# Decoder layer on one core: one PSUM bank for the turned probabilities of both heads, two banks for the query and key projections, and a new order of steps

## The chip, the cores and the metric

The kernel runs on one core of one Trainium2 chip. The metric is the device time in microseconds; before the change it is 413.04, the median of three runs (412.48 to 413.12). The core has a matrix engine (TensorE, PE in the profile, its weight loads as PEld), a vector engine (VectorE, DVE), an activation engine (ScalarE, ACT), GpSimd (POOL) and SyncE (SP), which issues most DMAs. Each works through its own instructions in the order written, and they wait for each other through semaphores. Matmul results go to PSUM, which has eight banks; this kernel uses all of them, and a bank must have been copied out before it is written again.

## The reference

```
x = x + attention(layernorm(x))        # 16 heads of 64, rmsnorm inside, softmax over 256 keys, w_out, b_out
x = x + cross(layernorm(x), ctx)       # one head of 128, 512 context rows
x = x + ffn(layernorm(x))              # 128 -> 512 -> 128 with fake quantisation:
                                       #   activations uint8, one scale for the whole tensor (max / 255)
                                       #   weights int8 per output channel (max |w| / 127)
```

x is 8 x 256 x 128, the context 8 x 512 x 128, all float32. The scale of the quantisation is taken over the whole tensor, so the feed-forward part can begin only when all eight batches have left the cross attention.

## The kernel before

The order of all work is written out by hand. A batch has eight **steps** (j = 0 to 7), one for each pair of heads; batch 0 is "first", batches 1 to 6 are "mid" and run in a loop of two batches a turn, batch 7 is "last". In a step TensorE does work for pairs at different stages: it projects queries and keys for the pair three ahead (`project_qk`, six matmuls, L435), makes the scores two ahead (`scores`, twelve, L442), turns the probabilities of this pair (`turn_probs`, four transposes a head, L454), adds the output projection of two pairs back (`project_out`, L471) and multiplies probabilities and values of the pair before (`values`, L462). Projection and scores keep float32 accuracy in three passes with a rounded part (hi) and a rest (lo): ACT copies the rounded part out of the bank (`split_hi`), VectorE subtracts for the rest (`split_lo`), and only then is the bank free.

Around it, for each head: VectorE takes the row maxima (`maxima`), ACT the exponentials with their sums (`exps`), VectorE inverts the sums (`invert_sums`), POOL scales the probabilities (`scale_probs`), TensorE turns them, and VectorE copies the turned ones out of PSUM (`keep_turned`). ACT copies the values' result out as oT (L771) before the output projection can read it.

Each step has two places for a **side task** on one bank, `side_bank`: place 0 after the projection, place 1 after the transposes. PLACE (L52) says which task stands where: W1, W3 (value projections of this batch), V0, V2 and TH (value projections and the transposed input of the next batch), and the cross attention of the batch before: TC (its context transposed), TX (xn2 transposed), QX, SX0, SX1 (scores), PX0, PX1 (transposed probabilities), UX0, UX1 and OX (results). A task waits until the one before it has left the bank (`side_free`). TX needs `xn2`: the output projection of the batch's last pair (in step 1 of the next batch), then on VectorE `residual`, `aggregate`, then POOL's `inverse_root`, then `normalise` at the head of step 2.

The banks are two for scores, two for turned probabilities (one a head), one each for q, side, o and acc. Before the steps begin, the first pairs borrow free banks: pair 1 projects into o_bank, pair 2 into acc_bank, and the scores of pair 1 lie in the two banks of the turned probabilities.

Behind the last batch come its last values, its cross attention in a written-out form, and the feed-forward part over four chunks of 512 tokens. There the second product gives yT, ACT adds the bias (L883), and `scale_back` (L682) multiplies by a diagonal matrix of the scale s2, which turns the chunk and scales it at once.

## Time and profile before

| | |
|---|---|
| time, median of 3 (lowest to highest) | 413.04 (412.48 to 413.12) |
| time of the profiled execution | 412.56 |
| its span | 410.4 |
| mean granted TensorE clock | 0.982 |
| TensorE busy | 382.6 (93%) |
| VectorE busy | 320.2 (78%) |
| ACT busy | 260.4 (63%) |
| POOL busy | 161.0 (39%) |
| start until the first projection of step 0 (batch 0) | 16.25 |
| first projection of batch 1 | 57.45 |
| first projection of batch 7 | 324.58 |
| last values of batch 7 | 362.72 |

Busy time is a share of the span, and a high share says only that an engine may be the bound. To see what a step costs, read the distances between the starts of groups on one engine's timeline, not the durations: the duration of a matmul group includes the tail of its pipeline, which overlaps with the next group.

### The profile page before, as it was taken

The numbers are of one execution on the slowest core, as the hardware profiler recorded it, in microseconds if no ns is written. First come the engines' busy times: TensorE is split into PE (matmuls) and PEld (weight loads), VectorE is DVE, ScalarE is ACT, GpSimd is POOL, SyncE is SP. The second block draws the span as 40 slices with busy tenths as digits, with TensorE's granted clock in tenths as the row PEclk, the third lists the DMA queues.
The fourth block names the chain that finished last, engine by engine and source line by source line (L and its number), as shares of the span: only waits on it lengthen the run. The fifth ranks groups of instructions, "written<-read, shape, count | busy, mean of one in ns | idle before, by whom it ended". The sixth has DMA issues, their size and how long they took to land.

```text
span 410.4 us, 9160 instructions
## 1 busy us (share of the span) xinstructions
PE 382.6 (93%) x3037; PEld 294.9 (72%) x3037; DVE 320.2 (78%) x779; ACT 260.4 (63%) x814; POOL 161.0 (39%) x177
## 2 busy tenths in 40 slices
PE   6799999999999999999999999999999999987775
PEld 6577877687777876787768777787688777765224
DVE  3596778868987798859887798779885979847893
ACT  3776566676657665765767665766576666825672
POOL 1355434452454343534445345435353443501000
PEclk9889999999999999999999999999999999999699
DMA  7400000001000010001000100001000000000003
GB/s 234 137 16 2 2 0 2 2 2 40 0 2 2 2 38 0 0 0 38 0 0 0 38 0 0 0 0 38 0 0 0 26 2 3 0 2 0 0 2 102
DMA packets 12310, 7.50 MB, mean 18 GB/s; under 512 B 1280, under 2 KB 11264, under 8 KB 12288
## 3 DMA queue, kind: packets, MB, share of 16 engines
q1 hardware_dynamic: 11856, 6.69, 5.5%
q10 hardware_dynamic: 432, 0.52, 0.4%
q8 instruction: 13, 0.21, 0.2%
q14 instruction: 9, 0.07, 0.1%
HBM read 6.16 MB, written 1.05 MB: 18 GB/s over the span
## 4 chain that ended last, share of the span: by engine, by line
PE 74%; DVE 10%; issue 8%; POOL 3%; ACT 3%; DMA 1%; DVEq 0%; POOLq 0%; ACTq 0%
PE o_bank L467 14%; PE pT L458 12%; PE score L448 12%; PE acc_bank L474 6%; PE q_bank L431 6%; PE q_bank L433 3%; PE q_bank L432 3%; PE side_bank L431 3%; PE side_bank L525 3%; PE side_bank L432 2%; PE side_bank L433 2%; DVE h_max L1221 2%; DVE negmax L899 2%; POOL rstd L1255 2%; PE side_bank L521 2%
## 5 line engine op out<-in xcount | busy, mean ns | idle before, releaser
L1264 POOL TENSOR_TENSOR prob<-prob,rinv 128x512 f32<-128x512 f32 x128 | 132.5, 1044 | 177.6 <-DVE rinv L903 177.5
L717 ACT ACTIVATE prob<-score,negmax 128x256 f32<-128x256 f32 x252 | 117.1, 475 | 79.1 <-DVE negmax L899 78.4
L899 DVE TENSOR_REDUCE negmax<-score 128x2 f32<-128x512 f32 x126 | 80.9, 683 | 43.7 <-PE score L448 43.6
L906 DVE COPY pT<-pT 128x512 f32<-128x512 f32 x128 | 86.4, 678 | 1.6
L458 PE MATMUL pT<-ident,prob 128*128 128x128 f32 x512 | 71.2, 282 | 0.1
L467 PE MATMUL o_bank<-pT,v_sb 128*64 128x256 f32 x512 | 69.4, 392 | 0.6 <-ACT oT L708 0.6
L458 PEld LDWEIGHTS pT<-ident,prob 128*128 128x128 f32 x512 | 55.6, 142 | 9.7 <-issue 0.9
L717 ACT ACTIVATION_READ_ACCUMULATOR prob<-score,negmax 128x1 f32 x252 | 51.8, 205 | 0.0
L708 ACT ACTIVATE q_hi<-q_bank 128x512 fp32r<-128x512 f32 x62 | 37.5, 604 | 17.7 <-PE q_bank L433 17.3
L448 PE MATMUL score<-q_hi 64*128 64x256 f32 x252 | 42.2, 331 | 2.1 <-ACT prob L717 2.1
L467 PEld LDWEIGHTS o_bank<-pT,v_sb 128*64 128x64 f32 x512 | 31.1, 136 | 17.8 <-issue 1.2
L431 PE MATMUL q_bank<-ht_hi,wqk_hi 128*128 128x256 f32 x124 | 41.3, 333 | 2.3 <-DVE q_lo L891 1.2
L891 DVE TENSOR_TENSOR q_lo<-q_bank,q_hi 128x512 fp32r<-128x512 f32 x62 | 42.2, 681 | 1.0 <-ACT q_hi L708 1.0
L431 PEld LDWEIGHTS q_bank<-ht_hi,wqk_hi 128*128 128x128 f32 x124 | 23.2, 187 | 26.2 <-DVE q_lo L891 12.6
L474 PE MATMUL acc_bank<-wo_sb,oT 128*128 128x128 f32 x256 | 39.0, 276 | 0.0
L448 PEld LDWEIGHTS score<-q_hi 64*128 64x128 f32 x252 | 23.6, 184 | 18.2 <-issue 13.5
L474 PEld LDWEIGHTS acc_bank<-wo_sb,oT 128*128 128x128 f32 x256 | 34.7, 191 | 1.6 <-issue 0.4
L448 PE MATMUL score<-q_lo,q_hi 64*128 64x256 f32 x252 | 35.8, 279 | 0.0
L448 PE MATMUL score<-q_hi,q_lo 64*128 64x256 f32 x252 | 35.6, 278 | 0.0
L433 PE MATMUL q_bank<-ht_hi,wqk_lo 128*128 128x256 f32 x124 | 34.9, 282 | 0.0
L432 PE MATMUL q_bank<-ht_lo,wqk_hi 128*128 128x256 f32 x124 | 34.9, 281 | 0.0
L1255 POOL TENSOR_TENSOR rstd<-veps,ln_pow 128x2 f32<-128x2 f32 x24 | 17.0, 710 | 41.5 <-DVE veps L922 40.8
(220 smaller groups left out, 616.8 us busy)
## 6 DMA issues: line engine op xcount, KB each, us to landing
c_sb<-in_ctx_dram SPq DMA_DIRECT2D x8, 256.0 KB, 2.9
x_sb<-in_x_dram SPq DMA_DIRECT2D x8, 128.0 KB, 2.7
out_dram<-xn_all SPq DMA_DIRECT2D x4, 256.0 KB, 2.3
big<-in_L_attn_wk_dram ACTq DMA_DIRECT2D x2, 256.0 KB, 4.7
big<-in_L_attn_wq_dram SPq DMA_DIRECT2D x2, 256.0 KB, 5.7
big<-in_L_attn_wv_dram SPq DMA_DIRECT2D x2, 256.0 KB, 6.3
wo_sb<-in_L_attn_w_out_dram SPq DMA_DIRECT2D x1, 512.0 KB, 7.7
w_sb<-in_L_ffn_w_dram SPq DMA_DIRECT2D x2, 256.0 KB, 4.5
```

The costliest lines, as they stand in the source:

```text
L431: nc.tensor.matmul(dst, lhs_hi, rhs_hi, start=True, stop=False)
L432: nc.tensor.matmul(dst, lhs_hi, rhs_lo, start=False, stop=False)
L433: return nc.tensor.matmul(dst, lhs_lo, rhs_hi, start=False, stop=True)
L448: last = nc.tensor.matmul(banks[r][:, t * S:(t + 1) * S], query[rows, parity, 0, t * P:(t + 1) * P], key[rows, parity, 1, :], start=(n == ...
L458: last = nc.tensor.transpose(pT_bank[r][:, kt * S + t * P:kt * S + (t + 1) * P], prob[:, slot, t, kt * P:(kt + 1) * P], ident[:])
L467: last = nc.tensor.matmul(o_bank[r * E:(r + 1) * E, 0:S], v_sb[:, vp, kt, h * E:(h + 1) * E], pT[:, slots[r], kt, :], start=(kt == 0), sto ...
L474: last = nc.tensor.matmul(acc_bank[:, t * D:(t + 1) * D], oT[:, pair % 2, t * P:(t + 1) * P], wo_sb[:, pair, :], start=(pair == 0 and t == 0),
L717: last = nc.scalar.activation(prob[:, slot, t, :], banks[r][:, t * S:(t + 1) * S], ACT.Exp, bias=negmax[:, slot, t:t + 1], scale=1.0, accu ...
L891: return nc.vector.tensor_tensor(dst, whole, hi.bitcast(F32), ALU.subtract)
L899: nc.vector.tensor_reduce(negmax[:, slot], banks[r][:].rearrange("p (t k) -> p t k", k=S), X_AXIS, ALU.max, negate=True).then_inc(max_done, 1)
L906: nc.vector.tensor_copy(pT[:, slot].rearrange("p k q -> p (k q)"), pT_bank[r][:]).then_inc(pT_done, 1)
L1264: nc.gpsimd.tensor_tensor(prob[:, slot], prob[:, slot], rinv[:, slot].unsqueeze(2).to_broadcast([P, QT, S]), ALU.mult).then_inc(prob_done, 1)
```

## The change

- `turned_bank` holds the turned probabilities of both heads. The second head's transposes move to the end of TensorE's step, behind `values`, and wait until the first head has been copied out (`pT_done`). VectorE copies the first head right behind both maxima, ahead of `split_lo`.
- `q_banks` are two banks used in turn. TensorE waits for `q_lo_done` before the scores and no longer before the projection.
- Side tasks: V2 of the next batch becomes W2 of this batch; UX0 and UX1 become one task UX with 256 columns; most tasks change place (PLACE).
- The last pair's output projection moves from behind step 1's transposes to before its scores; VectorE's `residual` moves before step 1's maxima, POOL's `inverse_root(1)` before its first scaling. The next batch's first `normalise` moves from step 0 to step 3, `cross_norm` from the middle to the end of step 7.
- Start: pair 1 projects into the second q bank, pair 2 into `turned_bank`; the scores of pair 1 lie in o_bank and acc_bank; the scores of pair 2 wait for the exponentials of pair 0 only. The second halves of the projection weights are split earlier, that of the value weights later.
- Last batch: the feed-forward weights' maxima move from step 2 to step 0, ACT's rounding copies from step 4 to step 1, VectorE's from step 5 to step 3; TL moves to step 7.
- Feed-forward: each second product waits tile by tile; ACT applies scale and scaled bias at once; `turn_back` transposes with the identity matrix.

The core of the diff, where the first `step` is TensorE's and the second VectorE's:

```diff
-PLACE = {(0, 0): "TC", (0, 1): "W1", (1, 0): "W3", (1, 1): "TH", (2, 0): "V0", (2, 1): "TX", (3, 0): "QX",
-         (3, 1): "SX0", (4, 0): "SX1", (4, 1): "PX0", (5, 0): "PX1", (5, 1): "UX0", (6, 0): "UX1", (6, 1): "OX",
-         (7, 0): "V2"}
+PLACE = {(0, 0): "W2", (0, 1): "TC", (1, 0): "W1", (2, 0): "W3", (2, 1): "TX", (3, 0): "QX", (3, 1): "TH",
+         (4, 0): "SX0", (4, 1): "PX0", (5, 0): "SX1", (5, 1): "PX1", (6, 0): "UX", (6, 1): "OX", (7, 0): "V0"}
...
-        pT_bank = [bank("pT0"), bank("pT1")]
-        q_bank = bank("q_bank")
+        turned_bank = bank("turned_bank")
+        q_banks = [bank("q_bank0"), bank("q_bank1")]
+        pT_bank = [turned_bank, q_banks[1]]
...
             def step(kind, b, parity, i, j):
-                if more_scores:
-                    pe.wait_ge(q_lo_done, g + 3)
                 if more_q:
-                    project_qk((j + 3) % PAIRS, parity if j < PAIRS - 3 else 1 - parity)
+                    project_qk((j + 3) % PAIRS, parity if j < PAIRS - 3 else 1 - parity, q_banks[(j + 3) % 2])
                 if task := side_at(kind, j, 0):
                     side(kind, b, 1 - parity, i, task)
+                if cross and j == 1:
+                    pe.wait_ge(o_done, g - 1)
+                    project_out(PAIRS - 1)
                 if more_scores:
-                    pe.wait_ge(exp_done, 2 * g + 4)
+                    pe.wait_ge(q_lo_done, g + 3)
+                    pe.wait_ge(exp_done, 2 if kind == "first" and j == 0 else 2 * g + 4)
                     scores(j % 2)
                 pe.wait_ge(prob_done, 2 * g + 1)
-                wait(pe, pT_done, 2 * g - 1)
-                turn_probs(0, 2 * j % 8)
-                pe.wait_ge(prob_done, 2 * g + 2)
                 wait(pe, pT_done, 2 * g)
-                turn_probs(1, 2 * j % 8 + 1)
-                if task := side_at(kind, j, 1):
-                    side(kind, b, 1 - parity, i, task)
+                turn_probs(2 * j % 8)
...
-                if not (kind == "first" and j < 2):
+                if j != 1 and not (kind == "first" and j < 2):
                     project_out((j - 2) % PAIRS)
+                if task := side_at(kind, j, 1):
+                    side(kind, b, 1 - parity, i, task)
                 if not (kind == "first" and j < 1):
                     values((j - 1) % PAIRS, (slot, slot + 1), 1 - parity if j == 0 else parity)
+                pe.wait_ge(prob_done, 2 * g + 2)
+                pe.wait_ge(pT_done, 2 * g + 1)
+                turn_probs(2 * j % 8 + 1)
...
-                    last = nc.tensor.matmul(y_banks[n % 2][:, k * P:(k + 1) * P],
-                                            xrT[:, (4 * n + k) * P:(4 * n + k + 1) * P], s2_diag[:], start=True, stop=True)
+                    last = nc.tensor.transpose(y_banks[n % 2][:, k * P:(k + 1) * P],
+                                               xrT[:, (4 * n + k) * P:(4 * n + k + 1) * P], ident[:])
...
             def step(kind, b, parity, i, j):
+                if prepare and j == 3:
+                    normalise(0, tiles(xn1), tiles(x_sb[:, 1 - parity]), b + 2, xn1_done)
                 if task := side_at(kind, j, 0):
                     side(kind, b, 1 - parity, task)
+                if cross and j == 1:
+                    residual(b, 1 - parity)
                 if more_scores:
                     for r in range(2):
                         dve.wait_ge(score_raw, 2 * g + 5 + r)
                         maxima(r, (2 * j + 4 + r) % 8)
+                dve.wait_ge(pT_raw, 2 * g + 1)
+                keep_turned(2 * j % 4)
...
                 if ahead(kind, j, 3):
                     dve.wait_ge(q_hi_done, g + 4)
-                    split_lo((j + 3) % 2)
-                dve.wait_ge(pT_raw, 2 * g + 1)
-                keep_turned(0, 2 * j % 4)
+                    split_lo((j + 3) % 2, q_banks[(j + 3) % 2])
+                if task := side_at(kind, j, 1):
+                    side(kind, b, 1 - parity, task)
                 if more_scores:
                     dve.wait_ge(exp_done, 2 * g + 5)
                     invert_sums((2 * j + 4) % 8)
...
                 dve.wait_ge(pT_raw, 2 * g + 2)
-                keep_turned(1, 2 * j % 4 + 1)
+                keep_turned(2 * j % 4 + 1)
```

## Rows read from the trace of the kernel before

**Rows 1.** Stretches: busy microseconds (instructions) of each engine, granted TensorE clock, DMA share, GB/s

```profile
57.45:101.77 44.32, 43.31 (x364) 34.19 (x362) 35.15 (x86) 29.19 (x97) 19.88 (x21) 1.00 0.04 11
...
235.46:280.01 44.55, 43.53 (x363) 34.22 (x361) 36.25 (x89) 29.33 (x97) 19.87 (x21) 1.00 0.03 9
```

**Rows 2.** Waits of TensorE: microseconds in total, times, longest

```profile
PE side_bank L513 <- DVE xn L931: 7.5, 7, 1.5
```

**Rows 3.** Timeline, plain step 6 of batch 0: start, duration, engine, instruction group

```profile
48.16 0.39 PE L431 MATMUL q_bank<-ht_hi,wqk_hi 128*128 128x256 f32 x1
...
49.76 0.28 PE L448 MATMUL score<-q_hi,q_lo 64*128 64x256 f32 x2
...
49.97 1.09 PE L458 MATMUL pT<-ident,prob 128*128 128x128 f32 x8
...
50.08 1.29 DVE L899 TENSOR_REDUCE negmax<-score 128x2 f32<-128x512 f32 x2 [1.08 <-PE score L448]
...
50.90 0.61 PE L474 MATMUL acc_bank<-wo_sb,oT 128*128 128x128 f32 x4
...
51.28 0.68 DVE L891 TENSOR_TENSOR q_lo<-q_bank,q_hi 128x512 fp32r<-128x512 f32 x1
...
51.44 1.08 PE L467 MATMUL o_bank<-pT,v_sb 128*64 128x256 f32 x8
...
51.88 0.68 DVE L906 COPY pT<-pT 128x512 f32<-128x512 f32 x1
...
52.45 0.39 PE L431 MATMUL q_bank<-ht_hi,wqk_hi 128*128 128x256 f32 x1
```

**Rows 4.** Timeline, step 2 of a middle batch and what leads to TX

```profile
246.35 0.39 PE L431 MATMUL q_bank<-ht_hi,wqk_hi 128*128 128x256 f32 x1
...
246.61 0.42 DVE L950 TENSOR_TENSOR x_sb<-acc_bank,xb_sb 128x256 f32<-128x256 f32 x1
...
247.67 0.69 DVE L906 COPY pT<-pT 128x512 f32<-128x512 f32 x1
...
249.45 1.04 POOL L1264 TENSOR_TENSOR prob<-prob,rinv 128x512 f32<-128x512 f32 x1
...
249.52 1.30 DVE L931 TENSOR_SCALAR xn<-x_sb,mv,rstd 128x128 f32<-128x128 f32 x2 [0.67 <-POOL rstd L1255]
...
250.97 0.41 PE L513 MATMUL side_bank<-ident,xn 128*128 128x128 f32 x2 [1.01 <-DVE xn L931]
...
252.77 0.39 PE L431 MATMUL q_bank<-ht_hi,wqk_hi 128*128 128x256 f32 x1
```

**Rows 5.** Timeline, last batch: transposes, then SX0, then the output projection

```profile
343.53 1.09 PE L458 MATMUL pT<-ident,prob 128*128 128x128 f32 x8
...
345.16 0.61 PE L474 MATMUL acc_bank<-wo_sb,oT 128*128 128x128 f32 x4
```

**Rows 6.** Timeline: UX0, one group of eight instructions

```profile
266.93 1.06 PE L525 MATMUL side_bank<-x_pT,c_sb 128*128 128x128 f32 x8
```

**Rows 7.** Timeline of the start, with one stretch as in rows 1

```profile
19.36 0.39 PE L448 MATMUL score<-q_hi 64*128 64x256 f32 x2 [2.14 <-ACT prob L717]
...
20.10:23.50 3.40, 3.40 (x17) 2.62 (x13) 3.12 (x9) 1.86 (x6) 2.03 (x4) 0.53 0.02 5
...
24.43 0.39 PE L431 MATMUL q_bank<-ht_hi,wqk_hi 128*128 128x256 f32 x1 [0.81 <-DVE q_lo L891]
```

**Rows 8.** Timeline, last batch: last matmul of the last scores, and the last values

```profile
353.51 0.28 PE L448 MATMUL score<-q_hi,q_lo 64*128 64x256 f32 x2
...
362.72 1.08 PE L467 MATMUL o_bank<-pT,v_sb 128*64 128x256 f32 x8 [0.57 <-ACT oT L708]
```

**Rows 9.** Line L686 by tile (min/median/max ns), and timeline of the end

```profile
L686 PEld LDWEIGHTS side_bank<-s_diag,xrT x16: 186/192/192, 401.1 to 405.5; 128*128 128x128 f32 x16
...
401.14 1.13 PE L686 MATMUL side_bank<-s_diag,xrT 128*128 128x128 f32 x8 [0.71 <-ACT xrT L883]
...
406.94 0.69 DVE L1246 TENSOR_TENSOR xn_all<-score,x_all 128x512 f32<-128x512 f32 x1 [0.35 <-PE score L686]
```

More of the change, by code:

```diff
@@ L101, in side_before @@
     def side_before(kind, b):
-        return before(kind, b, [*PREPARE, *LAST_PLACE.values(), "XW", "XE"])
+        return before(kind, b, [*PREPARE, *LAST_PLACE.values(), "XW", "XE", "V2"])
     def side_index(kind, b, task):
@@ L433, in three_passes, with project_qk @@
                 return nc.tensor.matmul(dst, lhs_lo, rhs_hi, start=False, stop=True)
-            def project_qk(pair, hp, bank=q_bank):
+            def project_qk(pair, hp, bank):
                 for n in range(2):
@@ L524, in side @@
                     for kt in range(CT):
-                        last = nc.tensor.matmul(side_bank[:, 0:P], c_sb[:, p, kt, :], x_pT[:, kt, int(task[2]), :],
+                        last = nc.tensor.matmul(side_bank[:, 0:S], c_sb[:, p, kt, :],
+                                                x_pT[:, kt].rearrange("p t q -> p (t q)"),
                                                 start=(kt == 0), stop=(kt == CT - 1))
@@ L749, in side @@
                 else:
[L750 to L751 removed]
+                    copy(uT[:], side_bank[:, 0:S]).then_inc(side_free, 1)
             def step(kind, b, parity, i, j):
@@ L771, in step @@
                     copy(oT[:, (j - 1) % 2], o_bank[:, 0:S]).then_inc(o_done, 1)
-                if kind == "last" and j == 4:
+                if kind == "last" and j == 1:
                     act.wait_ge(w_inv_done, 1)
@@ L1062, in step @@
                     invert_sums((2 * j + 4) % 8)
-                if (task := side_at(kind, j, 1)) and not early:
-                    side(kind, b, 1 - parity, task)
-                if cross and j == 1:
-                    residual(b, 1 - parity)
-                if kind == "mid" and j == PAIRS - 2:
-                    dve.wait_ge(side_free, side_index(kind, b, "OX") + 1)
-                dve.wait_ge(pT_raw, 2 * g + 2)
-                keep_turned(1, 2 * j % 4 + 1)
-                if prepare and j == 0:
-                    normalise(0, tiles(xn1), tiles(x_sb[:, 1 - parity]), b + 2, xn1_done)
-                if cross and j == 1:
-                    aggregate(1, b, *PLAIN_NORM)
+                dve.wait_ge(pT_raw, 2 * g + 2)
+                keep_turned(2 * j % 4 + 1)
                 if kind == "mid" and j == PAIRS - 2:
                     statistics(2, x2_of(b), b)
+                if kind == "mid" and j == PAIRS - 1:
+                    cross_norm(b)
                 if kind == "last":
@@ L1282, in step @@
                     inverse_root(2, b)
+                if cross and j == 1:
+                    inverse_root(1, b)
                 if more_scores:
```

123 lines of the change are left out of this document (59 added, 64 removed).

## Prediction, made before the changed kernel was run

> Times below are microseconds of the profiled execution. A step is what one pass of the hand-written order does for one pair of heads; I name the eight steps of a batch 0 to 7, and s is the start of the last score matmul of a step, the clock on which I place the other engines.
>
> **What bounds the kernel now.** I read the stretches first. In a middle batch TensorE is busy 43.53 of 44.55 and VectorE 36.25 [rows 1]: TensorE is the bound, and VectorE, in a fixed order, has some 8 us of slack. Then the waits of TensorE: one stands out, the transposes of xn2, which wait for VectorE seven times, 7.5 in all [rows 2]. Then one plain step, because the change cuts it up: it lasts 4.29 (48.16 to 52.45), made of projection and scores (48.16 to 49.97, 1.81), eight transposes (0.93), output projection (0.54) and values (1.01) [rows 3]. What a side task adds comes from [rows 5]: eight transposes and a 512-column side task take 1.63, so the task is 0.70; two transposes are 0.23, four 0.46 [rows 3]. With these I count what each step of a middle batch needs. Step 1 needs 5.22 and step 2 needs 4.30 + 0.70 + 0.22 = 5.22, but step 2 lasts 252.77 - 246.35 = 6.42 [rows 4]: 1.20 lost to the xn2 chain. The needs of a middle batch are 8 x 4.29 = 34.3, six 512-column tasks 4.2, four tasks of four transposes or their like 1.8, two of two 0.45, QX 0.55, UX0 and UX1 0.89 each (1.06 with the last one's tail [rows 6]): 43.1. Of 44.55 that leaves 0.24 beside the 1.20; it sits in step 0, where W1 waits for the side bank. So at most 1.45 of 44.55 can be had in a middle batch unless the matmuls themselves get cheaper.
>
> **The xn2 chain.** Today the batch's last output projection comes after step 1's transposes, and VectorE's residual comes at 246.61, statistics and all until 247.67, then POOL's power, and the normalise is done at 250.82, TensorE following at 250.97 [rows 4]. After the change that projection stands ahead of step 1's scores, some 2.9 before its old place, and the residual ahead of the maxima. The normalise then ends about 0.3 before step 2's maxima are due, and TX, later in its step, finds it done. Gain 1.20 a batch, and W1 no longer waits for the context split: 0.24.
>
> **One bank for both heads.** The second head's four transposes must wait until VectorE has copied the first head out, and that copy now stands behind both maxima. On the clock of s: the maxima start at s+0.32 (50.08 against 49.76) and the next instruction 1.20 later (51.28), so the copy runs from s+1.52 to s+2.20 (0.68 as at 51.88) [rows 3]. A result of VectorE reaches TensorE about 0.15 after its end (250.82 to 250.97) [rows 4]: the second head may start at s+2.35. TensorE is there at s + 0.21 + 0.47 (four transposes) + 0.54 + 1.01 = s+2.23 [rows 3], plus a side task of the second place (0.23 to 0.46).
> - Steps 0, 4, 5, 6 (four transposes or OX beside): cover 0.34, no wait. Steps 2 and 3 (two transposes): cover 0.11.
> - Step 7 (nothing beside): 0.12 plus VectorE's lateness, which today is 0.2 there; I take 0.20.
> - Step 1: the projection has left, nothing is beside, and the residual holds the maxima up. TensorE is there at s+1.77. The residual waits for the projection, ends with its statistics 1.06 later [rows 4], and puts the maxima at s+0.47, so the second head starts at s+2.50. Wait 0.73. This is where half of the gain goes.
> - The normalise of the next batch now stands at the head of step 3, beside POOL's scaling. Beside such a scaling (249.45, 1.04 long) one took 1.30 and ended after it [rows 4]. In step 3 the scaling, the bias addition and the second scaling follow each other, so the maxima may be late by 0 to 1.0; I take 0.2, near what one blocked instruction costs, and with step 0 that is 0.15 of wait.
> The Trainium skill, SBUF — State Buffer, section "Who interferes with whom", says that the loser of the port pair which VectorE and GpSimd share is blocked for the whole instruction. By that rule, if each of three POOL instructions in a row won, step 3 would lose up to 0.9 a batch, and the sum would be 5 us worse; the row shows one blocked turn only.
> New waits in a middle batch: 0.73 + 0.20 + 0.15 = 1.08.
>
> **Two projection banks, and what now follows what.** The wait for q_lo moves from the projection to the scores. No middle step was held by it, so it gives nothing there. The projection now follows transposes, not values. After values its first matmul takes 0.10 more than a plain interval [rows 3]; a 512-column task after transposes shows no such loss (1.63 = 0.93 + 0.70) [rows 5]. So a step is cheaper by 0 to 0.10; I take 0.04, as a short matmul hides a weight load less well: 0.32 a batch. Transposes after values replace a projection after values: taken as equal, within 0.02. UX0 and UX1 become one group of eight instructions with twice the columns; one group of today lasts 1.06 with its tail [rows 6], the same columns pass, so nothing, within 0.1 a batch. One ACT copy in place of two is off the path.
>
> Middle batch: -1.20 - 0.24 + 1.08 - 0.32 = -0.68, and six of them -4.1; the first of them lasts 44.32 and has no wait of 0.24 to lose [rows 1]: **-3.9**. Bounds: new waits from 0.85 to 2.0 and the bubble from 0 to 0.10 give -1.1 to +0.5 a batch, -6.6 to +3.
>
> **Start and first batch.** Scores of pair 2 wait 2.14 for the exponentials of pair 1 [rows 7]; they now need those of pair 0 alone, gain 2. But the first head's copy stands behind VectorE's inversion of the last exponentials, the low half of the value weights (whose high half ACT now makes last), the statistics and both maxima: the last exponentials end near 19.3, as today, where the scores are released at 19.36 [rows 7]; the weights' high half takes ACT until 20.0, VectorE's low half until 20.8, inversion and statistics until 21.6, two maxima and the copy 1.9 more, so the copy ends near 23.5 and TensorE stands idle from 18.6 to 23.6. The projection of step 1 then starts near 24.1 instead of 24.43 [rows 7]. Step 1 waits again about 0.6 for the copy, but the 0.70 of W1 has moved into it from step 0. Net to the third step, about 0. An idle stretch of 2.14 before it was followed by a stretch at a granted 0.53, near the lower level, 1.2 GHz [rows 7], in which eight transposes took 1.62 instead of 0.93; after an idle stretch of five I expect the same once more behind the restart: 0 to 2.0, I take 1.2. Five steps with nothing beside: +0.5, bubble -0.3. Sum **+1.4**, from -0.3 to +3.
>
> **Last batch.** It gains the wait on xn2, 1.5 here, the longest of the seven [rows 2]. It pays: the feed-forward weights' maxima now follow step 0's copy, four instructions of some 1.8 together, and push step 1's residual by 0.5, wait 1.25 there; the quantised weights follow step 3 (1.5), wait 0.4 in step 4; W2 is 0.70 more than the pair that it replaces, but V2's share has left the first batch, where W1 and W3 moved one step on. From step 5 on no projection or scores stand between one head's transposes and the next head's, so each must wait for the previous copy: second head's last transpose + 0.28 + 0.68 + 0.15 makes 1.0 in step 6, 0.6 in step 7, and 1.1 before the last values. Today from the last scores (353.51) to the last values (362.72) it is 9.21 [rows 8]; I get 11.2 for the same stretch, of which 0.44 is PX1 moved in. Sum **+2.1**, from +0.8 to +4.
>
> **Behind it.** One UX group and one copy in place of two with a wait each: -0.3, then the xn2 chain ends last. In the feed-forward network the output transposes are true transposes, one instruction each instead of two: eight instructions of 0.192 weight load a chunk become four [rows 9]. The first still starts when ACT is free, 401.14. From there: four transposes 0.47, chunk 2 0.90, 0.47, chunk 3 0.90, then ACT's 0.7 for the last chunk and its 0.47: the last addition starts at 405.6 instead of 406.94 [rows 9]. The finer waits on the quantised tiles let the first product start 0.5 earlier, which ACT hides; it would cost nothing without that cover. **-1.3** (-0.9 to -1.5).
>
> **Sum.** -3.9 + 1.4 + 2.1 - 0.3 - 1.3 = -2.0. The profiled execution took 412.56 (span 410.4 and 2.2 around it), 0.48 under the median of 413.04; 413.04 - 2.0 = **411.0**.
>
> **Rivals.**
> 1. *The bubble goes entirely.* If projection after transposes runs as tightly as the 512-column task, a further 0.06 in each of 61 steps is 3.7, and 407.3. For: [rows 5]. Against: its matmuls are half as long.
> 2. *The ends eat the middle.* Start at +3, last batch at +3.5 by the serial copies, middle -3.9: 413.0 + 3 + 3.5 - 3.9 - 1.6 = 414.0; with each half that far, 412.5, no change. For: VectorE's queue at both ends is the densest. Against: the start was already held at 24.43 by the same engine.
> 3. *The copy comes late in every step* (slower). Place: VectorE's order, copy behind both maxima. If it ends later by L than s+2.20, steps 1 and 7 lose L, steps 2 and 3 L less 0.11, in the first batch five steps lose L: about 4 L in each batch of eight, 30 L in all. From L = 0.07 the gain is gone; at L = 0.2 it is 411 + 6 = 417. For: VectorE is 81% busy and POOL blocks its normalise. Against: the maxima start within 0.2 of their due time in most steps.
> 4. *The chain doesn't do what it says*: TX still waits, since POOL's power comes behind a scaling. Price 0.5 a batch, 414.
>
> **Chances.** Forecast (409 to 412.2) 0.40; rival 1 0.20; rival 2 0.19; rival 3 0.15; rival 4 0.06. The measurement can tell about 0.2% (0.8 us) from no change. Faster: forecast and rival 1, 0.60. Same: rival 2, whose time lies about the bound, 0.19. Slower: rivals 3 and 4, 0.21. The forecast alone spans 409.0 to 412.2; eight times in ten, 406.8 to 415.5.
>
> **What would show it.** Step 2 of a middle batch near 5.2 with no wait on xn2; a gap of 0.7 before the second head's transposes in step 1, put down to VectorE's copy; a middle batch of 43.9; the second scores at 17 and TensorE idle until 23.6; the last values 2 later after the last scores; one transpose instruction each at the end. It is wrong if the copy waits appear in steps 0 and 4 to 6, if middle batches exceed 44.5, or if the granted clock falls in a middle batch.

## The result, and the profile after

| | before | after | forecast |
|---|---|---|---|
| median of 15 runs each, same chip | 412.68 (411.26 to 414.19) | 410.02 (408.40 to 411.14) | 411.0 from 413.04 |
| difference of the medians | | -2.66 | -2.0 |
| ratio | | 0.994, 95% interval 0.9924 to 0.9957 | 0.995 |
| profiled execution: time, span | 412.56, 410.4 | 409.33, 407.5 | |
| a middle batch (mean of the six) | 44.55 (44.52) | 43.90 (43.84) | 43.87 |

The changed kernel is a little faster, by 1.8 to 3.1. The forecast of 411.0 and its range (406.8 to 415.5) hold the time, and faster was the likeliest of the three cases.

Stretches of the changed kernel: the first middle batch, two others and the last batch up to the last values (busy time and number of instructions of each engine, then granted clock; they answer to [rows 1]):

```profile
core 0: us, PE busy (x) PEld busy (x) DVE busy (x) ACT busy (x) POOL busy (x), PEclk, DMA share, GB/s
58.10:101.75 43.65, 42.70 (x356) 33.10 (x355) 35.93 (x87) 29.26 (x96) 19.92 (x21) 1.00 0.04 11
189.56:233.44 43.88, 42.94 (x356) 33.17 (x355) 37.06 (x90) 29.36 (x97) 19.95 (x21) 1.00 0.03 9
233.44:277.36 43.92, 42.89 (x355) 33.11 (x354) 37.03 (x89) 29.18 (x96) 19.95 (x21) 1.00 0.03 9
321.14:361.40 40.26, 36.55 (x301) 27.33 (x299) 32.67 (x73) 25.03 (x82) 16.02 (x16) 1.00 0.00 1
```

TensorE is still the bound, at the full granted clock, and idles 0.9 to 1.0 in a middle batch. Its waits in the whole kernel (total, times, longest), where [rows 2] had the transposes of xn2 with 7.5 in seven:

```profile
PE turned_bank L462 <- DVE pT L912: 12.7, 17, 4.8
PE acc_bank L663 <- DVE fmax L1199: 2.7, 1, 2.7
PE o_bank L471 <- DVE pT L912: 0.8, 1, 0.8
PE side_bank L525 <- ACT x_prob L736: 0.6, 1, 0.6
```

The wait on xn2 is gone from the batches, and the second head's transposes (line 462) wait for VectorE's copy (line 912) instead, 17 times. In which steps, the timeline says. Step 1 of the batch that starts at 233.44, TensorE and VectorE (start, duration, then the idle time ahead of it and what ended it); here s, the start of the last score matmul, is 241.89:

```profile
240.66 0.61 PE L478 MATMUL acc_bank<-wo_sb,oT 128*128 128x128 f32 x4
241.36 0.42 DVE L956 TENSOR_TENSOR x_sb<-acc_bank,xb_sb 128x256 f32<-128x256 f32 x1 [0.82 <-issue]
241.89 0.28 PE L452 MATMUL score<-q_hi,q_lo 64*128 64x256 f32 x2
242.43 1.29 DVE L905 TENSOR_REDUCE negmax<-score 128x2 f32<-128x512 f32 x2
242.69 1.08 PE L471 MATMUL o_bank<-pT,v_sb 128*64 128x256 f32 x8
243.64 0.68 DVE L912 COPY pT<-turned_bank 128x512 f32<-128x512 f32 x1
244.46 0.63 PE L462 MATMUL turned_bank<-ident,prob 128*128 128x128 f32 x4 [0.69 <-DVE pT L912]
245.94 1.62 DVE L937 TENSOR_SCALAR xn<-x_sb,mv,rstd 128x128 f32<-128x128 f32 x2
```

The moved projection, the residual behind it, both maxima, the copy, and only then the second head: 0.69 idle, where I had 0.73. The normalise is through at 247.56, before step 2's transposes of xn2 are due (they start at 248.28).

The steps of this batch, from the starts of their projections (233.44, 238.83, 244.85, 250.02, 254.98, 260.35, 265.75, 272.18, 277.36), last 5.39, 6.02, 5.17, 4.96, 5.37, 5.40, 6.43 and 5.18; in the same batch before they were 5.67, 5.22, 6.42, 5.53, 5.44, 5.64, 5.63 and 5.00. Step 2 is down from 6.42 to 5.17, step 1 up from 5.22 to 6.02. The output projection stood in step 1 before as well, so it adds nothing there; TH with its 0.22 has left. What has come is the wait of 0.69, and 0.34 at W1, the value projection in place 0, which finds the side bank still in use:

```profile
239.13 0.68 DVE L897 TENSOR_TENSOR cT_lo<-side_bank,cT_hi 128x512 fp32r<-128x512 f32 x1
239.51 0.28 PE L437 MATMUL q_bank<-ht_hi,wqk_lo 128*128 128x256 f32 x1
239.86 0.50 PE L435 MATMUL side_bank<-wv_hi,ht_hi 128*128 128x512 f32 x1
240.20 0.40 PE L436 MATMUL side_bank<-wv_lo,ht_hi 128*128 128x512 f32 x1
```

VectorE's last read ends at 239.81. The matmul starts 0.35 after the one before it, where 0.12 is the distance without a wait, and the next follows after 0.34 instead of 0.23. Step 6 takes the UX group that before was split over steps 5 and 6.

The start and the end, where the change lost:

```profile
19.94 1.29 DVE L905 TENSOR_REDUCE negmax<-score 128x2 f32<-128x512 f32 x2
21.14 0.68 DVE L912 COPY pT<-turned_bank 128x512 f32<-128x512 f32 x1
21.97 1.09 PE L462 MATMUL turned_bank<-ident,prob 128*128 128x128 f32 x4 [4.80 <-DVE pT L912]
...
354.39 0.63 PE L462 MATMUL turned_bank<-ident,prob 128*128 128x128 f32 x4 [0.88 <-DVE pT L912]
357.94 0.63 PE L462 MATMUL turned_bank<-ident,prob 128*128 128x128 f32 x4 [0.44 <-DVE pT L912]
361.40 1.08 PE L471 MATMUL o_bank<-pT,v_sb 128*64 128x256 f32 x8 [0.78 <-DVE pT L912]
```

A stretch of 4.80 in which TensorE has nothing, against the 2.14 of [rows 7]; and three waits in a row, 2.10 in all, between the last scores and the last values, where [rows 8] had one, of 0.57.

### The profile page after: what moved, and what is told of

Read it like the earlier page. It is cut to its first block, busy times and chain, and to the rows that moved or that the text cites. A ratio compares the mean times of both kernels' runs of the same rounds, so it can differ in the third digit from the quotient of the medians.

```text
span 407.5 us, 9018 instructions
## 1 busy us (share of the span) xinstructions
PE 377.0 (93%) x2965; PEld 284.3 (70%) x2965; DVE 326.2 (80%) x779; ACT 260.4 (64%) x807; POOL 161.6 (40%) x177
## 4 chain that ended last, share of the span: by engine, by line
PE 60%; DVE 22%; issue 11%; ACT 3%; DMA 1%; DVEq 1%; POOL 1%; POOLq 0%; ACTq 0%
PE turned_bank L462 14%; PE score L452 10%; PE o_bank L471 10%; DVE pT L912 6%; DVE negmax L905 5%; PE acc_bank L478 4%; PE q_bank L435 3%; PE q_bank L436 3%; PE q_bank L437 3%; PE side_bank L529 3%; DVE h_max L1222 2%; DVE stats L918 2%; PE side_bank L436 2%; PE side_bank L435 2%; PE side_bank L437 2%
## 5 line engine op out<-in xcount | busy, mean ns | idle before, releaser
L912 DVE COPY pT<-turned_bank 128x512 f32<-128x512 f32 x128 | 87.3, 682 | 13.0 <-PE turned_bank L462 11.2
L462 PE MATMUL turned_bank<-ident,prob 128*128 128x128 f32 x512 | 83.7, 286 | 13.3 <-DVE pT L912 12.7
L462 PEld LDWEIGHTS turned_bank<-ident,prob 128*128 128x128 f32 x512 | 54.0, 142 | 47.7 <-issue 38.4
L716 ACT ACTIVATE oT<-o_bank 128x256 f32<-128x256 f32 x64 | 25.6, 400 | 6.6 <-PE o_bank L471 6.6
```

Of the source, the lines that this page charges most:

```text
L462: last = nc.tensor.transpose(turned_bank[:, kt * S + t * P:kt * S + (t + 1) * P], prob[:, slot, t, kt * P:(kt + 1) * P], ident[:])
L716: return nc.scalar.activation(dst, src, ACT.Copy, **kw)
L912: nc.vector.tensor_copy(pT[:, slot].rearrange("p k q -> p (k q)"), turned_bank[:]).then_inc(pT_done, 1)
```

## The experiments

All are compared with the changed kernel, 410.02, unless said otherwise. The interval of a ratio is 0.4 to 0.6% wide, 1.6 to 2.6 us; where a trace gives the stretch in question, that decides.

**1. The copy between the maxima.** Does its place set the waits?

```diff
-                    for r in range(2):
-                        dve.wait_ge(score_raw, 2 * g + 5 + r)
-                        maxima(r, (2 * j + 4 + r) % 8)
+                    dve.wait_ge(score_raw, 2 * g + 5)
+                    maxima(0, (2 * j + 4) % 8)
                 dve.wait_ge(pT_raw, 2 * g + 1)
                 keep_turned(2 * j % 4)
+                if more_scores:
+                    dve.wait_ge(score_raw, 2 * g + 6)
+                    maxima(1, (2 * j + 5) % 8)
```

> The changed kernel with one edit: VectorE copies the first head out between the two maxima instead of behind both, in every step. My theory (the copy's place behind the maxima sets the second head's start, and TensorE is otherwise the bound): the copy ends 0.68 earlier. In a middle batch the wait of 0.69 in step 1 falls to about 0.2 (the residual still holds the first maximum up) and that of 0.2 in step 7 goes: 0.7 a batch less, 4.2 over six. In the first batch the idle stretch ahead of the second head's transposes is 0.7 shorter and step 1 has no wait (0.4), in the last batch step 1 gains 0.6. Together -6 us against the changed kernel: 404. Rival (the second maximum is what matters, because the exponentials of the second head and with them the next scores come 0.68 later): TensorE waits for prob in front of the scores instead, and the time stays at 410 or rises to 413.

Measured 406.88 (ratio to before 0.987, 0.9847 to 0.9893). The gain has the sign of my theory and half its size, -3.1. The waits for the copy are all gone from the middle batches:

```profile
PE turned_bank L462 <- DVE pT L912: 5.8, 4, 4.2
```

but the six middle batches fall only from 263.04 to 261.72, 0.2 each, where I had 0.7. Steps 3 and 4 became longer, 4.95 to 5.09 and 5.40 to 5.62, and step 1 fell only by 0.3 (5.85 and 6.02 to 5.47 and 5.73), since W1 now starts 0.40 and 0.64 after the matmul before it, not 0.18 and 0.35. Neither theory had that. The timeline of step 4, where the scores of the cross attention follow the projection:

```profile
209.00 0.47 DVE L966 SCALAR_TENSOR_TENSOR ht_lo<-side_bank,scale_d,ht_hi 128x256 fp32r<-128x256 f32 x1
209.29 0.28 PE L437 MATMUL q_bank<-ht_hi,wqk_lo 128*128 128x256 f32 x1
209.52 0.50 PE L435 MATMUL side_bank<-cT_hi,qx_hi 128*128 128x512 f32 x1
```

VectorE's last read of the side bank ends at 209.47, TensorE's next write begins at 209.52, 0.23 after the start of the projection's last matmul; before the edit it was 0.13 (211.62 to 211.75). The matmul behind it follows after 0.34 instead of 0.23, so that the step loses the 0.22. The second maximum has pushed the low half of the side task 0.6 back, and the side bank is now late. The rival (scores waiting for exponentials) is out: no such wait stands in the list but the one of the first step. The last batch gained nothing (40.49 against 40.26): its wait in step 1 fell from 0.92 to 0.32, but its transposes of xn2 now wait 0.59 in step 2.

**2. The copy one instruction later**, behind the projection's low half: what does a late copy cost?

```diff
-                dve.wait_ge(pT_raw, 2 * g + 1)
-                keep_turned(2 * j % 4)
...
                     split_lo((j + 3) % 2, q_banks[(j + 3) % 2])
+                dve.wait_ge(pT_raw, 2 * g + 1)
+                keep_turned(2 * j % 4)
```

> The changed kernel with one edit: the first head's copy stands one 0.68 us instruction later still, behind the low half of the new projection. This prices a late copy. My theory (cover as in the prediction: 0.34 in steps 0, 4, 5, 6, 0.11 in steps 2 and 3, nothing in steps 1 and 7): a middle batch loses 4 x 0.34 + 2 x 0.57 + 2 x 0.68 = 3.9, together with the two ends about +31 us against the changed kernel, 441. Rival (steps 0 and 4 to 6 have more cover than that, so that only four steps feel it): 2.5 a batch, +20, 430. If it costs under 5 the one bank was never a risk.

442.49 (ratio 1.0721, 1.0697 to 1.0745): +32.5, my theory's 31, not the rival's 20. A middle batch (here from step 7 to step 7) lasts 48.00, 4.1 more, where I had 3.9:

```profile
107.30:155.30 48.00, 43.09 (x357) 33.07 (x355) 37.58 (x88) 29.22 (x95) 20.00 (x21) 1.00 0.04 10
```

TensorE's work is the same, and it waits 62 times, once in nearly each of the 64 steps. So rival 3 was a real danger: 0.68 of lateness turns -2.7 into +30. But only the sum of the covers is right, not the steps'. In one batch, from the lengths of its steps against the changed kernel's:

| step | 0 | 1 | 2 | 3 | 4 | 5 | 6 | 7 |
|---|---|---|---|---|---|---|---|---|
| loss by the prediction's covers | 0.34 | 0.68 | 0.57 | 0.57 | 0.34 | 0.34 | 0.34 | 0.68 |
| measured | 0.63 | 0.81 | 0.43 | 1.12 | 0.22 | 0.22 | 0.21 | 0.55 |

Steps 4 to 6 have more cover than I gave them, steps 0, 1 and 3 lose more than the copy's 0.68 less their cover, and the errors cancel to 0.3.

**3. The projection moved back**, with its residual, aggregation and power: is the chain of xn2 worth what it costs in step 1?

```diff
-                if cross and j == 1:
-                    pe.wait_ge(o_done, g - 1)
-                    project_out(PAIRS - 1)
...
-                if j != 1 and not (kind == "first" and j < 2):
+                if not (kind == "first" and j < 2):
```

> The changed kernel with one part undone: in step 1 the last output projection stands behind the first head's transposes again, the residual and the statistics behind the side task's place, and GpSimd's power behind both scalings. My theory: the transposes of xn2 in step 2 wait about 1.1 again, and in exchange the wait of 0.69 for the copy in step 1 falls to about 0.1, because the projection covers it. Net +0.4 to +0.5 a batch, +3 over seven batches: 413. Rival A (the wait in step 1 comes from VectorE's residual ahead of the maxima and stays whatever covers it, or grows): +1.1 a batch, 418. Rival B (the whole gain of the middle batches comes from the closed gap behind the values, and moving the projection is worth nothing net): 410.

417.43 (ratio 1.0134, 1.0113 to 1.0155), +7.4. That is rival A's number, though not its reason. The wait in step 1 did go, as my theory had it (the step lasts 5.17 to 5.39, not 5.85 to 6.02). But step 2 lasts 7.00:

```profile
207.20 0.60 DVE L933 TENSOR_SCALAR xn<-x_sb,mv,rstd 128x128 f32<-128x128 f32 x2 [1.80 <-POOL rstd L1253]
207.72 1.28 DVE L901 TENSOR_REDUCE negmax<-score 128x2 f32<-128x512 f32 x2
207.94 0.41 PE L517 MATMUL side_bank<-ident,xn 128*128 128x128 f32 x2 [1.22 <-DVE xn L933]
208.91 0.68 DVE L908 COPY pT<-turned_bank 128x512 f32<-128x512 f32 x1
209.74 0.63 PE L462 MATMUL turned_bank<-ident,prob 128*128 128x128 f32 x4 [0.37 <-DVE pT L908]
```

VectorE waits 1.80 for the power, at the head of the step, and everything behind it is late: TensorE first waits 1.22 for xn2, then 0.37 more for the copy. With one bank a late VectorE is paid for twice. The six middle batches take 270.74, 45.1 each and 1.3 more than in the changed kernel; I had counted the first wait only.

**4. Another bank for the second head at the end of the last batch.**

```diff
+                if kind == "last" and j >= 5:
+                    if j == 5:
+                        pe.wait_ge(q_lo_done, B * PAIRS)
+                    turn_probs(2 * j % 8 + 1, q_banks[0])
```

> The changed kernel with one edit, in the last batch alone: from its step 5 on, where no projection is left, the second head's transposes go into the other projection bank, so that one head's transposes need not wait for the copy of the head before. My theory (the 2.1 that the last batch lost is this chain of transposes and copies, 0.88 + 0.44 + 0.78 of waits in the trace): the stretch from the last scores to the last values falls from 11.24 to 9.2, -2.0, 408.0. Rival (the values wait for the copies whatever bank they come from): -0.8 at most, 409.2.

408.98 (ratio 0.9918, 0.9887 to 0.995), between the two. In the trace the waits of 0.88 and 0.44 are gone, that of 0.78 is not:

```profile
361.39 1.08 PE L471 MATMUL o_bank<-pT,v_sb 128*64 128x256 f32 x8 [0.78 <-DVE pT L919]
```

It was never the bank's: the last values need the last head's copy, and nothing is left to do meanwhile. The kernel before had a wait at this place too, 0.57, there for ScalarE's oT. From the last scores to the last values it is 9.80 (351.59 to 361.39) against 11.24 (350.16 to 361.40): -1.4 of the -2.0.

**5. The old end of the feed-forward network**, on the changed kernel.

```diff
-                    last = nc.tensor.transpose(y_banks[n % 2][:, k * P:(k + 1) * P],
-                                               xrT[:, (4 * n + k) * P:(4 * n + k + 1) * P], ident[:])
+                    last = nc.tensor.matmul(y_banks[n % 2][:, k * P:(k + 1) * P],
+                                            xrT[:, (4 * n + k) * P:(4 * n + k + 1) * P], s2_diag[:], start=True, stop=True)
```

> The changed kernel with the last transposes of the feed-forward network made as before, by four fp32 products a chunk with the diagonal of s2 in place of four true transposes; everything else stays. My theory: the products weigh twice as many instructions and twice the weight loads in a chain that nothing hides, +1.2 to +1.5, 411.3. Rival (the end is set by ScalarE and VectorE, and the transposes hide): 0 to +0.3, 410.2.

411.51 (ratio 0.9971, 0.9955 to 0.9987), +1.5; in the traces the stretch from the scale of h to the last addition is 9.24 in the changed kernel (394.86 to 404.10) and 10.57 with the old products (396.31 to 406.88): 1.33. The rival is out. The last two additions of the changed kernel, where [rows 9] had one at 406.94:

```profile
403.01 0.69 DVE L1248 TENSOR_TENSOR xn_all<-side_bank,x_all 128x512 f32<-128x512 f32 x1 [0.65 <-PE side_bank L695]
404.10 0.69 DVE L1248 TENSOR_TENSOR xn_all<-score,x_all 128x512 f32<-128x512 f32 x1 [0.40 <-PE score L695]
```

**6. The start**: VectorE's low half of the value weights, and the statistics of the next rows, behind the first step's maxima and copy instead of ahead.

> The changed kernel with one edit at its start: VectorE's low half of the value weights and the statistics of the next rows, which stand ahead of the first step's maxima and copy, follow them. My theory (TensorE's idle stretch of 4.80 ahead of the first step's second head is VectorE's queue): the maxima start at 17.1 instead of 19.9, the copy ends near 18.9, the second head is turned near 19.1 instead of 21.97, the weights are still in time for the side task at 20.3, -2.9: 407.1. Rival (the granted clock decides: the stretch at the lower level then starts earlier or lasts longer, or the side task and the next scores wait for the moved work): -1 or less, 409 or more.

407.41 (ratio 0.9877, 0.9849 to 0.9906), -2.6. The idle stretch is 2.71:

```profile
21.59 0.63 PE L462 MATMUL turned_bank<-ident,prob 128*128 128x128 f32 x4 [2.71 <-DVE pT L912]
```

So of the 4.80, 2.1 was this work in VectorE's queue. This profile has a stretch at the lower clock near the start that the changed kernel's lacks (see the last section); against the profile of experiment 4, which has it as well and starts alike, the time from the first projection to the first middle batch fell from 50.89 to 47.84, 3.0. No wait but the two for the copy (2.71, and 0.36 in step 1) is left between step 0's scores and the first middle batch.

**7. The feed-forward weights' work back in its old places** in the last batch (e8_old_weights in later texts).

> The changed kernel with the feed-forward weights' maxima and quantising in the last batch where they stood before (VectorE behind steps 2, 3 and 5, ScalarE behind step 4, in place of 0, 3 and 1). My theory (they put 0.25 on the wait in step 1, and 0.4 to 0.56 on that in step 4): -0.3 to -0.8, 409.5. Rival (they move other waits in as they move these out): no change, 410.

409.18 (ratio 0.9927, 0.9906 to 0.9948), which by itself is not clear of 410.02. In the traces the last batch up to the last values is 39.77 against 40.26: the waits of steps 1 and 4 fell from 0.92 to 0.60 and from 0.56 to 0.23, and one of 0.27 came in step 3. Net 0.5; both readings hold in part.

**8. Four edits together** (e7_all in later texts): those of 1, 4 and 6, and on VectorE the low half of the transposed side tasks ahead of the projection's low half, which answers what experiment 1 found.

```diff
+                early = side_at(kind, j, 1) in ("TC", "TX", "TH")
+                if early:
+                    side(kind, b, 1 - parity, side_at(kind, j, 1))
                 if ahead(kind, j, 3):
                     dve.wait_ge(q_hi_done, g + 4)
                     split_lo((j + 3) % 2, q_banks[(j + 3) % 2])
```

> Four edits on the changed kernel: the copy between the two maxima, the low halves of the transposed side tasks ahead of the low half of the projection on VectorE, the start of e6_start, and the bank of e4_last_bank. My theory (with the copy between the maxima alone, the side bank was handed back 0.6 later, which cost 0.14 in step 3 and 0.22 in step 4; the low halves first give that back): a middle batch of 43.3 instead of 43.9 (43.6 with the copy between alone), so -3.6 there, -3 at the start, -2 in the last batch: 401.5. Rival (the projection's low half then comes late for the scores, which wait instead): middle batches at 43.6 or more, 404.

402.70 (ratio 0.9777, 0.9749 to 0.9805). A middle batch lasts 43.25 (43.30 in the mean), as my theory had it; step 4 is back at 5.41, and step 1 down at 5.10 to 5.25. The side bank was the cause. Step 3 became 5.34, with one more turn of the same kind:

```profile
201.69 1.31 DVE L944 TENSOR_SCALAR xn<-x_sb,mv,rstd 128x128 f32<-128x128 f32 x2
202.92 0.47 DVE L986 SCALAR_TENSOR_TENSOR qx_lo<-side_bank,qx_bias,qx_hi 128x256 fp32r<-128x256 f32 x1
203.52 0.43 PE L491 MATMUL side_bank<-ident,xn 128*128 128x128 f32 x2 [0.28 <-DVE qx_lo L986]
```

The last batch gave only 0.8 (39.49 against 40.26) where my sum had 2. The 1.4 of experiment 4 is in it, and so is the loss that experiment 1 had shown: the rounding copies of the feed-forward weights, moved to step 1 by the change, keep ScalarE from its copy of the side bank, and TX waits.

```profile
326.58 1.89 ACT L723 ACTIVATE w_t<-w_sb,w_inv 128x128 f32<-128x128 f32 x5
329.49 0.44 PE L517 MATMUL side_bank<-ident,xn 128*128 128x128 f32 x2 [0.59 <-ACT v_sb L723]
```

**9. The moved projection alone, on the kernel before.** Did the gain need the new use of the banks?

```diff
+                if kind != "first" and j == 1:
+                    pe.wait_ge(o_done, g - 1)
+                    project_out(PAIRS - 1)
                 if more_scores:
                     pe.wait_ge(exp_done, 2 * g + 4)
                     scores(j % 2)
```

(with VectorE's residual and aggregation and GpSimd's power at the places that they have in the changed kernel)

> The kernel before with one part of the change alone: in step 1 the last output projection stands ahead of the scores, the residual ahead of the maxima, the aggregation behind them and GpSimd's power ahead of both scalings. One projection bank and a bank for each head stay. It tells whether the banks' new use was needed for the gain. Theory A (needed): the wait of 1.2 on xn2 goes, but VectorE's low half of the projection now ends near s+2.7 in step 1, and the single projection bank is wanted at s+2.15: a new wait of 0.7 in its place. Net -0.5 a batch, 409. Theory B (not needed: the low half is in time): -1.2 a batch and -1.5 in the last, 404.

407.44 (ratio to before 0.9885, 0.9865 to 0.9905): between the theories, and faster than the changed kernel.

```profile
100.56:144.47 43.91, 43.50 (x364) 34.32 (x362) 36.23 (x89) 29.42 (x97) 19.92 (x21) 1.00 0.04 10
```

```profile
PE q_bank L431 <- DVE q_lo L894: 3.0, 9, 0.4
```

The new wait of theory A is there at the end of step 1 in each of seven batches (two of the nine are at the start), 0.33 in a middle batch and not 0.7. As much again is lost in step 2, where the matmuls' list of waits names nothing: VectorE's low half of TH, pushed back by the residual, leaves the side bank late.

```profile
244.04 0.47 DVE L963 SCALAR_TENSOR_TENSOR ht_lo<-side_bank,scale_d,ht_hi 128x256 fp32r<-128x256 f32 x1
244.56 0.50 PE L431 MATMUL side_bank<-wv_hi,ht_hi 128*128 128x512 f32 x1
```

That matmul starts 0.35 after the one before it, not 0.12, and step 2 lasts 5.54 where it needs 5.22. So a middle batch lasts 43.91, the same as the changed kernel's 43.90 (263.12 against 263.04 for six), but made differently: here TensorE is busy 43.50 and waits little, there it is busy 42.9 and waits 1.0. The new use of the banks does make TensorE's row of work shorter; its waits take that back.

**10. The best version**: the edits of 8, the weights' work as in 7, and the next rows' normalise in step 2, at a moment in which GpSimd is idle.

> The four edits of e7_all with two more: the feed-forward weights' work where it stood before (as in e8_old_weights), and the normalise of the next batch's rows from the head of step 3 to step 2, behind the low half of the projection, where GpSimd is idle. In the trace of e7_all step 3 lasts 5.34, since the normalise takes 1.31 beside GpSimd's scaling and the side bank comes free late; I expect 5.15 there (-0.2 a batch, -1.2 in all) and -0.7 in the last batch: 400.8 (402.7 for e7_all). Rival (the normalise, wherever it stands, delays the next copy by as much): 402.

398.77 (ratio 0.9691, 0.9664 to 0.9718), better than expected and the fastest of all, 3.1% under the kernel before.

```profile
97.19:140.12 42.93, 42.69 (x356) 33.10 (x355) 36.63 (x89) 29.20 (x96) 19.93 (x21) 1.00 0.04 11
```

```profile
199.91 0.59 DVE L944 TENSOR_SCALAR xn<-x_sb,mv,rstd 128x128 f32<-128x128 f32 x2
```

The normalise takes 0.59 where it took 1.31, step 3 lasts 5.03, and TensorE idles 0.24 in a middle batch. The six middle batches gain 1.9 on experiment 8 (259.79 to 257.87) where I had 1.2. The last batch up to its last values is 37.91 (312.13 to 350.04) against 39.49, 1.6 less where I had 0.7: with the weights' work back in its old places the wait of 0.59 is gone too, and that of 0.74 which stood in step 4. The two edits were not run apart.

**11. The kernel before with the moved projection and the new end of the feed-forward network**, banks as before: does the rest of the change cost what the parts say?

> The kernel before with the moved projection of e9_before_moved and the changed kernel's true transposes at the end of the feed-forward network; the banks as before. What then separates it from the changed kernel is the new use of the banks and what was moved with it. Theory (the new use of the banks is worth nothing in a middle batch and costs 1.7 at the start and 2 to 3 in the last batch, the parts add up): 407.4 - 1.3 = 406.1, some 4 under the changed kernel's 410.0. Rival (the tail's gain hangs on the new banks or on where the clock stands, or the middle batches of e9_before_moved were a chance of one profile): 407 or more.

405.76 (ratio to before 0.9832, 0.9808 to 0.9855), 4.3 under the changed kernel. From the scale of h to the last addition it is 9.24, and the middle batches are those of experiment 9.

## Why the prediction was right, and where not

The two profiles, term by term:

| term | forecast | measured |
|---|---|---|
| six middle batches | -3.9 | -4.1 (267.13 to 263.04) |
| start and first batch | +1.4 | +0.65; +0.9 to +2.2 like with like |
| last batch to the last values | +2.1 | +2.1 (38.14 to 40.26) |
| behind it | -0.3 | -0.3 (5.60 to 5.28) |
| end of the feed-forward network | -1.3 | -1.3 (10.57 to 9.24) |

- **The xn2 chain** held: step 2 lasts 5.17 as forecast (5.2), and its wait is gone. Rival 4 is out. The 0.3 to spare ahead of the maxima was not there: the projection stands 1.84 earlier in its step (1.83 against 3.67 from its start), not 2.9, and the normalise took 1.62 instead of 1.30; the maxima started right behind it, s+0.37 instead of s+0.32.
- **The one bank** held where it waits: 0.69 in step 1 (0.73; the 1.77 at which I had TensorE there should by my own parts be 1.69), 0.19 in step 7 (0.20), none in steps 0, 4, 5 and 6. Experiment 2 priced the covers at 4.1 a batch (3.9), right in the sum and wrong by steps. Half of the forecast's gain was expected to come back here, and it did.
- **Step 3** held too, though no view lists it: the copy ends at 254.44 and the second head's transposes start at 254.59, 0.15 behind it and 1.16 after the values' start, where it takes 1.02 without a wait. That is 0.14 of wait; I had 0.15 with step 0.
- **W1** was mis-sized. Its 0.24 was to vanish; it is gone from step 0, but W1 now stands in step 1 and waits there for the low half of the transposed context: in one batch that ends at 195.76 and the matmul starts at 195.82, which costs 0.17 with the late matmul behind it, in the next it ends at 239.81 and the matmul starts at 239.86, 0.34. The step 1 lengths of 5.85 and 6.02 differ by this.
- **QX** was mis-sized the other way. The 0.55 came from a row in which QX itself was late by the xn2 chain (its first matmul at 253.67 is 0.20 after the one before it, and 0.05 after VectorE's last read of the side bank); in the changed kernel it adds 0.36. So step 3 lasts 4.96 with its wait, where the prediction's needs give 5.07 without one. That the middle batch came out at 43.90 against 43.87 is in part luck: W1 and QX cancel.
- **The bubble**: with no wait in it a step without side task lasts 4.26 (experiments 1, 8 and 10, first batch), where it lasted 4.29. I had taken 0.04 of 0 to 0.10. Rival 1, that all of it goes, is out. In the changed kernel itself these steps last 4.32, since the copy is just late in them (in step 6 it ends at 48.23, the second head starts at 48.38, 1.11 after the values' start instead of 1.02). The lower bound of the middle batches is mis-added: 0.85 of waits and the whole bubble give -1.4 a batch, not -1.1.
- **The last batch** came out at the forecast for the reasons given, each a little off: 0.88, 0.44 and 0.78 at its end where I had 1.0, 0.6 and 1.1; step 1 at 0.92 instead of 1.25; step 4 at 0.56 instead of 0.4, and there it is PX0, waiting for ScalarE's exponentials, not the second head.
- **The end**: the first transposes start 4.77 behind the scale of h in both profiles, as I had it, and the last addition 4.47 behind them (399.63 to 404.10), not 5.80. From 401.14 that is my 405.6, though the parts that I listed add up to 405.05.
- **The start** is the term with the weakest footing. Its mechanism was right: released by the copy at 21.97, an idle stretch of 4.80 (I had 5.0, 1.6 later on the clock), then a stretch at the lower clock, in which step 1 lasts 6.95. But the profile of before had a stretch of that kind earlier on which the profile of after has not; it cost 1.5 up to step 0 and hid part of the loss. The stretch behind the idle time varies as well: in experiment 3, whose start is that of the changed kernel, the clock fell between 18 and 19 and rose between 25 and 26, not between 20 and 21 and between 27 and 28, and step 1 lasts 6.17. From the first projection to the first middle batch:

| | with the early stretch | without |
|---|---|---|
| start of before | 48.71 (before), 49.22 (experiment 11) | 47.64 (experiment 9) |
| start of after | 50.89 (4), 50.88 (5) | 49.38 (after), 49.38 (7), 48.57 (3) |

Like with like the loss is 1.7 to 2.2 with it and 0.9 to 1.7 without; the means of three and five profiles differ by 1.3, near the 1.4 of the forecast. The weak step of the prediction is that I compared with one execution there, and took its clock for the kernel's.

With the start like for like the terms add up to -2.7 to -1.4, with the mean of the profiles to -2.3; the medians say -2.66 with an interval of -1.8 to -3.1. They agree so far; how often each kernel has the early stretch at the lower clock would make it sharper, and these runs don't settle it.

What the prediction didn't ask is which part of the change earns the gain. Experiments 9 and 11 say: the moved projection alone earns all of the middle batches' 0.64 (43.91 against 43.90), the transposes at the end earn 1.3, and the new use of the banks, with what moved along with it, earns nothing in a middle batch and costs about 4 (410.02 against 405.76), at the start and in the last batch. With VectorE's order made for it a middle batch is 42.93 (42.98 in the mean), 0.9 to 1.0 under what the old banks gave. But the same care was not given to the old banks: experiment 9 still loses 0.33 and 0.32 a batch to VectorE's order, and without these it would be near 43.3 (an estimate from its rows, not run). So perhaps 0.3 of that 1.0 is the banks', and what they are worth at their best is open.

## What to carry to other kernels

When two users are put on one buffer, the copy that frees it joins the critical path: place it in its engine's order as if it were the bottleneck's instruction, and count the cover of each step with and without side work, first of all in the steps at both ends, where there is none. When a queue is reordered, the next thing to be late is what the moved work stood ahead of; here it was the side bank, and only step lengths showed it, since a wait that is just met leaves no idle time in the matmuls' list and still cost 0.1 to 0.3 here. And of a change with several parts, run each part alone: the best one may be hidden by the others.

## What the runs showed that I had not expected

**A stretch at the lower clock that comes and goes.** In the profile of the kernel before, TensorE ran at a mean granted clock of 0.72 between 8 and 14; in that of the changed kernel it ran at 1.00 over the same time:

```profile
8.00:14.00 6.00, 5.26 (x32) 4.64 (x34) 2.56 (x4) 2.48 (x5) 0.00 (x0) 0.72 0.98 252
```

```profile
8.00:14.00 6.00, 5.28 (x48) 4.65 (x49) 4.38 (x8) 4.48 (x11) 0.00 (x0) 1.00 1.03 260
```

The first is of before, the second of after. From the first projection to that of step 0 it is 7.51 against 6.01 with the code of before (before, experiment 9), and 6.98 against 5.48 with that of after (experiments 4 and 7). In the profile of before the clock stood at 1.00 until past 9, at 0.5 (1.2 GHz) from 10 to 13, and at 1.00 (2.4 GHz) again from 14. TensorE had idled for 0.42 ahead of 7.15 and for 1.15 ahead of 8.74, and was busy without a gap from there on, through the fall; in the changed kernel's profile it had idled nearly as much there (busy 0.75 of the 2.00 from 7 to 9, against 0.70), and the clock did not fall. So the idle time alone does not decide it, and what does stays open. Seven of the thirteen profiles have this stretch. The times of one kernel spread over 1.6 to 3.4; those of before lie in two clumps (411.3 to 411.8 and 412.5 to 413.4, and one of 414.2). The Trainium skill, TensorE: Matmul & The Clock Gate, section "The HAM clock gate", says that the number of matmuls at the lower clock at a kernel's start varies from run to run; the profiles here agree in that, with 0.72 or 1.00 over the same stretch, though this stretch is not at the very start: from 2 to 8 all of them were granted 1.00. For a change of 1 us at the start, one profile a side is not enough.

**The normalise and GpSimd.** The same kind of pair took 0.59 with GpSimd idle (experiment 10), 1.28 and 1.31 in step 3 beside a scaling and the bias addition behind it, and 1.62 in step 2 of the changed kernel beside two scalings in a row. The Trainium skill, SBUF — State Buffer, section "Who interferes with whom", says that the loser of the shared port pair is blocked; the trace agrees: the pair of 1.62 ends at 247.56, 0.08 behind the second scaling. Moving the pair from the head of step 3 into step 2 made step 3 shorter by 0.3 (5.34 to 5.03).
